# Turning the rows of the first and the last batch on TensorE in an attention and expert kernel, with new lists of the steps

## The chip, the cores and the metric

One core of a Trainium2 chip runs the whole program. Its engines each take their own queue of instructions in order: TensorE (PE, products; its loads of stationary data are PEld), VectorE (DVE), ScalarE (ACT), GpSimd (POOL) and the sync engine (SP), which issues DMAs. The metric is the device time of one execution in microseconds, the median of several runs.

## The reference

The input is 8 batches of 512 rows of 256 values in float32. A linear attention (no softmax, so keys and values can be multiplied first) and a mixture of experts each stand between two layer norms:

```
x = x + ln(attn(ln(x)))
    qkv = x @ Wqkv.T + b                 # 32 heads of 8
    ctx = q @ (k.T @ v) per head, then a group norm per head over (8, 512)
    return ctx @ out_w.T + out_b
x = x + ln(ffn(ln(x)))
    ffn(x) = silu(x @ gate.T) * (x @ up.T) @ down.T      # 704 hidden
    shared expert on all rows + top 2 of 8 experts by softmax(x @ gate_w.T)
```

## The kernel before

Products of float32 values are made from halves in float16: each operand is scaled and kept as a high and a low part, and three products (high x high, high x low, low x high) are summed (TERMS). TensorE wants the summed dimension on the partitions, so normalised rows have to be turned. For that ScalarE writes the high part of a batch's rows and VectorE the low part (steps turn1 and turn2, into rows1 and rows2), and SP issues four transposing DMAs (L421 into xq for the attention, L429 into xhl_v for router and shared expert).

The program has three stages. **START and eight rounds**: START computes batch 0's keys, values and state and its attention, and the first half of batch 1. Round b, for b from 1 to 6, goes through ORDER: the second half of batch b (ctx, group norm, out, lno, x2, ln2, turn2, logits), the first half of batch b + 1 (ln1_stats, ln1_apply, turn1, q, kv, state; FIRST_HALF), the shared expert for batch b - 1 (two tiles of 256 rows, each with six chunks: G is gate and up on TensorE, H the silu, product and split on ScalarE and VectorE, D down on TensorE), and the layout of expert b's weights from float32 (prep_max to prep). LAST_ORDER is round 7, without a first half and with routing steps. **TAIL** holds the shared expert for batch 7 and the routing: ranks (route_slots, route_order, route_positions), one-hot rows (one_hots on VectorE and GpSimd) that TensorE multiplies into index lists (invert), and route_indices. **Routed tiles**: 39 tiles of 256 gathered rows. GpSimd gathers (gather_x), SP turns (turn_x, L493), TensorE works, ScalarE copies out (y_out, L709), GpSimd scatters with addition (L628). Finished batches are normalised between the tiles; the last one after them.

What sets the order is the lists, written out by hand: every engine runs through the same PROGRAM and emits only its own part of each step, so the lists set each queue, and semaphores hold the engines together. G of chunk n waits until VectorE has made the product of chunk n - 2 (h_made, two PSUM banks), D of chunk n until its low half is there (lo_made), which VectorE makes in H of chunk n + 1. Attention has four PSUM banks (BANK); bank_ready waits for the last reader. In round b SP issues in this order: xres, turn1(b + 1), the store of x2, the store of a shared tile, turn2(b), the store of rows2 to xn2_d, the load of the next x, the next weights. xhl_v has two places by the parity of the batch: the tile xhl for odd ones and a part of the free weight slot 7 (spare) for even ones. xhl is also the place of the turned gathered tiles (xt16).

## Time and profile before

| | us |
|---|---|
| median of 3 runs (885.25 to 888.62) | 886.62 |
| the profiled execution | 888.74 |
| its span, first to last instruction | 887.0 |
| TensorE busy | 787.4 |
| VectorE busy | 586.4 |
| ScalarE busy | 483.7 |
| GpSimd busy | 291.1 |

The profile is of one execution. Busy time is summed per engine; the rows further down tell when each was busy, what an engine waited for, and the granted clock of TensorE, 1.00 being its high level.

### The profile page before, as it was taken

Reading aid. Unit: us, or ns where it says so; the run is one execution under the profiler, and the core shown is the slowest. Engines: PE = TensorE matmul, PEld = TensorE weight load, DVE = VectorE, ACT = ScalarE, POOL = GpSimd, SP = SyncE. Lnnn points to the kernel's source line nnn. Section 1 sums busy time; section 2 is a strip of 40 time slices with the busy share of each in tenths; the row PEclk is TensorE's granted clock in tenths of the full one; section 3 lists DMA queues with packets and bytes.
Section 4 is the critical chain, followed back from the end, with each engine's and each line's share of the span. In section 5 each row is a group of like instructions: output and inputs, shape, how many; then the busy total and the mean of one; then the engine's idle time right before and its main releaser. Section 6 shows DMA issues by size and latency. Waiting matters only on the chain.

```text
span 887.0 us, 21062 instructions
## 1 busy us (share of the span) xinstructions
PE 787.4 (89%) x6573; PEld 634.3 (72%) x6574; DVE 586.4 (66%) x1579; ACT 483.7 (55%) x1056; POOL 291.1 (33%) x316
## 2 busy tenths in 40 slices
PE   0757999999999999667799999999999999999990
PEld 0334767777666767545578888888888888888880
DVE  7163888888978887899477644455555555555552
ACT  1225575766656576622365655555555555656561
POOL 3010101010001000025245555555555555555532
PEclk9977999999999999979899999999999999999995
DMA  5125344536262625340324457766454646464723
GB/s 193 43 66 174 76 132 143 160 108 203 66 208 61 208 66 179 84 119 13 79 55 74 74 96 74 120 75 144 72 143 72 143 74 143 75 142 73 145 36 89
DMA packets 124307, 95.35 MB, mean 107 GB/s; under 512 B 85504, under 2 KB 115968, under 8 KB 123072
## 3 DMA queue, kind: packets, MB, share of 16 engines
q1 hardware_dynamic: 109264, 73.70, 30.6%
q0 software_dynamic: 14976, 20.78, 15.9%
q8 instruction: 39, 0.64, 0.3%
q14 instruction: 28, 0.23, 0.1%
HBM read 48.70 MB, written 27.39 MB: 86 GB/s over the span
## 4 chain that ended last, share of the span: by engine, by line
PE 72%; DVE 13%; DMA 4%; SPq 3%; ACT 3%; issue 3%; POOL 1%; ACTq 0%; DVEq 0%; POOLq 0%
PE ps L856 40%; PE ps L871 19%; PE ps L952 4%; SPq L429 3%; PE ps L911 2%; PE ps L937 2%; PE ps L917 2%; DVE mx L1173 2%; DVE hf L1144 2%; DMA wgu<-wgu 1%; DVE hT L1154 1%; DVE wdn L1440 1%; DMA xhl<-wgu 1%; DMA acc_d<-ysb,gst 1%; DVE st L1124 1%
## 5 line engine op out<-in xcount | busy, mean ns | idle before, releaser
L856 PE MATMUL ps<-xhl,wgu 128*128 128x256 f16 x3102 | 388.0, 275 | 12.3 <-DVE hf L1144 6.4
L856 PEld LDWEIGHTS ps<-xhl,wgu 128*128 (+1 forms) x3102 | 304.3, 99 | 55.0 <-issue 9.7
L1144 DVE SCALAR_TENSOR_TENSOR hf<-ps,sc,silu 128x256 f32<-128x256 f32 x330 | 159.6, 484 | 198.0 <-ACT silu L679 142.4
L871 PE MATMUL ps<-wdn,hT 128*128 (+1 forms) x1870 | 253.9, 274 | 1.6 <-DVE hT L1154 1.2
L679 ACT ACTIVATE silu<-ps,sc 128x256 f32<-128x256 f32 x275 | 130.1, 474 | 221.3 <-PE ps L856 206.9
L871 PEld LDWEIGHTS ps<-wdn,hT 128*128 128x128 f16 x1870 | 182.4, 98 | 25.7 <-DVE hT L1154 1.7
L628 POOL DMA_INDIRECT acc_d<-ysb,gst x78 | 128.7, 1650 | 44.5 <-POOL gst L624 30.9
L561 POOL TENSOR_TENSOR rstd<-ve,mhalf 128x4 f32<-128x4 f32 (+1 forms) x32 | 31.2, 974 | 322.2 <-DVE ve L1129 168.4
L693 ACT CAST hT<-hf 128x256 f16<-128x256 f32 x275 | 109.6, 398 | 17.9 <-DVE hf L1144 16.6
L1154 DVE TENSOR_TENSOR hT<-hf,hT 128x256 f16<-128x256 f32 x275 | 115.0, 418 | 1.7
L617 POOL DMA_INDIRECT attw<-xn_d,gst x78 | 80.8, 1035 | 44.5 <-POOL gst L613 32.6
L856 PE MATMUL ps<-wgu 128*128 128x256 f16 x528 | 64.8, 276 | 5.2 <-DVE hf L1144 5.2
L856 PEld LDWEIGHTS ps<-wgu 128*128 128x128 f16 x528 | 51.4, 100 | 16.6 <-DVE hf L1144 6.2
L917 PE MATMUL ps<-attw,att 128*128 128x512 f16 x192 | 47.0, 381 | 0.0
L624 POOL COPY gst<-ones 128x2 int32 (+1 forms) x39 | 8.5, 219 | 105.7 <-ACT ysb L709 105.7
L952 PE MATMUL ps<-attw,att 128*128 128x256 f32 x128 | 37.2, 415 | 3.1 <-DVE att L1335 3.1
L682 ACT ACTIVATE silu<-ps,sc 64x256 f32<-64x256 f32 x55 | 25.7, 468 | 25.9 <-PE ps L856 24.1
L911 PE MATMUL ps<-att,attw 128*128 128x512 f16 x96 | 26.3, 432 | 14.4 <-DMA att<-wdn 14.4
L709 ACT ACTIVATE ysb<-ps,yw 128x256 f32<-128x256 f32 x78 | 32.7, 472 | 3.4 <-DMA acc_d<-ysb,gst 3.4
L917 PEld LDWEIGHTS ps<-attw,att 128*128 128x128 f16 x192 | 17.9, 98 | 18.9 <-issue 0.8
L1204 DVE SCALAR_TENSOR_TENSOR wgu<-wgu,pw 128x1408 f16<-128x1408 f32 x16 | 26.4, 1682 | 7.0 <-ACT wgu L727 7.0
L753 ACT ACTIVATE att<-ps,colg 128x512 f32<-128x512 f32 x32 | 21.6, 684 | 15.5 <-PE ps L922 15.5
(227 smaller groups left out, 745.8 us busy)
## 6 DMA issues: line engine op xcount, KB each, us to landing
wgu<-in_gu SPq DMA_DIRECT2D x8, 1408.0 KB, 6.2
att<-in_x SPq DMA_DIRECT2D x16, 512.0 KB, 5.2
wdn<-in_dn SPq DMA_DIRECT2D x8, 768.0 KB, 8.3
x_d<-att SPq DMA_DIRECT2D x8, 512.0 KB, 3.0
xn_d<-wgu SPq DMA_DIRECT2D x8, 512.0 KB, 3.4
acc_d<-ysb SPq DMA_DIRECT2D x16, 256.0 KB, 3.2
att<-x_d SPq DMA_DIRECT2D x8, 512.0 KB
att<-acc_d SPq DMA_DIRECT2D x8, 512.0 KB, 4.4
```

The costliest lines, as they stand in the source:

```text
L617: g.indirect_dma_start(xg[:, r, t, :], None, xn2_d[:, :], bass.IndirectOffsetOnAxis(ap=idxc[:, 2 * r + t:2 * r + t + 1], axis=0)).then_inc ...
L628: g.indirect_dma_start(acc_d, bass.IndirectOffsetOnAxis(ap=idxc[:, 4 + t:5 + t], axis=0), ysb[:, t * D:(t + 1) * D], None, compute_op=ALU. ...
L679: a.activation(silu[:, c % 2 * TW:(c % 2 + 1) * TW], gu_ps[c % 2][:, 0:TW], ACT.Silu, scale=scale_of(slot, 0)).then_inc(silu_made, 1)
L693: a.copy(o, h).then_inc(hi_made, 1)
L709: ins = a.activation(ysb[:, tt * D:(tt + 1) * D], y_bank(u, tt), ACT.Copy, scale=by)
L856: ins = te.matmul(o, slot_gu(slot, hw, k, j), x(hx, k), start=(n == 0), stop=(n == len(TERMS) - 1))
L871: ins = te.matmul(y_bank(u, tt), h(hh), slot_dn(slot, c, hw), start=(c == 0 and n == 0 and tt == 0), stop=(c == FC - 1 and n == 1 and tt = ...
L911: ins = te.matmul(att_bank(QU + m)[:, :], wqkvT[:, hw, k, m * P:(m + 1) * P], xq[:, hx, k, :], start=(n == 0), stop=(n == len(TERMS) - 1))
L917: te.matmul(att_bank(KV_USES[t])[:, :], xq[:, hx, k, t * P:(t + 1) * P], wqkvT[:, hw, k, D:3 * D], start=(n == 0), stop=False)
L952: te.matmul(att_bank(OUT + h)[:, (t % 2) * D:(t % 2 + 1) * D], qT[:, k, t * P:(t + 1) * P], woT[:, k, :], start=(k == 0), stop=False)
L1144: v.scalar_tensor_tensor(out=hf[lo:P, c % 2 * TW:(c % 2 + 1) * TW], in0=up, scalar=scale_of(slot, 1, lo, P), in1=silu[lo:P, c % 2 * TW:(c ...
L1154: v.tensor_tensor(lo, h, hi, ALU.subtract).then_inc(lo_made, 1)
```

## The change

Batches 0 and 1 in the first norm (PE_FIRST) and batches 0 and 7 in the second (PE_SECOND) are turned by TensorE: eight transposes of 128x128 float32 blocks into two PSUM banks (turn, TURN1 and TURN2). ScalarE then writes the high and VectorE the low part from PSUM straight into xq (step turn1_out) or xhl_v (step xhl). The rows in float16 are still made for batch 0 and 7's second norm (step rows2, the former turn2), since xn2_d needs them, but no transposing DMA is issued. The other batches are turned by DMAs as before. The two places of xhl_v are swapped, so batch 7 is in the weight slot; the one-hot rows oh_hi move behind it. turn_x of the first two tiles now waits only for the gate and up products up to tile 13 of the shared expert, and the store of shared tile 15 goes behind them. The load of the last batch's sums is issued in two halves with a semaphore each. In a routed tile y_out is issued ahead of the normalising step of the same chunk, and in the last tile one chunk earlier. All four lists are new.

```
-ORDER = [("ctx",), ("G", 0), ("ctx_out",), ("channel_stats",), ("G", 1), ("H", 0), ("group_mean",), ("H", 1), ("G", 2), ("group_var",),
-         ("H", 2), ("D", 0), ("ctx_norm",), ("ln1_stats",), ("G", 3), ("G", 4), ("out",), ("H", 3), ("G", 5), ("ln1_apply",), ("H", 4),
-         ("D", 1), ("G", 6), ("turn1",), ("D", 2), ("H", 5), ("lno_stats",), ("G", 7), ("H", 6), ("D", 3), ("H", 7), ("lno_apply",),
...
+ORDER = [("ctx",), ("ctx_out",), ("G", 0), ("channel_stats",), ("H", 0), ("G", 1), ("group_mean",), ("G", 2), ("H", 1), ("ln1_stats",),
+         ("H", 2), ("group_var",), ("D", 0), ("G", 3), ("H", 3), ("ln1_apply",), ("D", 1), ("ctx_norm",), ("D", 2), ("G", 4), ("turn1",),
+         ("G", 5), ("out",), ("H", 4), ("H", 5), ("G", 6), ("D", 3), ("G", 7), ("prep_max", 0), ("G", 8), ("lno_stats",), ("H", 6),
+         ("q",), ("lno_apply",), ("q_out",), ("x2",), ("H", 7), ("kv", 0), ("H", 8), ("D", 4), ("kv_out", 0), ("D", 5), ("ln2_apply",),
...
+
+def turned_before(b, by_pe):
+
+    n = sum(c < b for c in by_pe)
+    return n, b - n
...
-CTX, GMEAN, GVAR, OUT, QU, STATE, LOGIT = 0, 2, 3, 4, 8, 16, 17
+CTX, GMEAN, GVAR, OUT, TURN1, QU, TURN2, STATE, LOGIT = 0, 2, 3, 4, 6, 8, 14, 16, 17
 KV_USES = [10, 11, 12, 13]
-BANK = {CTX: 0, CTX + 1: 1, GMEAN: 2, GVAR: 3, OUT: 0, OUT + 1: 1, QU: 2, QU + 1: 3,
-        10: 0, 11: 1, 12: 2, 13: 3, STATE: 2, LOGIT: 3}
-USES_FIRST = [QU, QU + 1] + KV_USES + [STATE]
+BANK = {CTX: 0, CTX + 1: 1, GMEAN: 2, GVAR: 3, OUT: 0, OUT + 1: 1, TURN1: 2, TURN1 + 1: 3, QU: 2, QU + 1: 3,
+        10: 0, 11: 1, 12: 2, 13: 3, TURN2: 0, TURN2 + 1: 1, STATE: 2, LOGIT: 3}
...
-        xhl_v = [a.rearrange("p (h k s) -> p h k s", h=2, k=KD) for a in (spare[:, 0:2 * KD * S], xhl[:, :])]
+        xhl_v = [a.rearrange("p (h k s) -> p h k s", h=2, k=KD) for a in (xhl[:, :], spare[:, 0:2 * KD * S])]
...
-                if b < B - 1:
+                if b < B - 1 and b + 1 not in PE_FIRST:
                     turn1(b + 1)
...
-                turn2(b)
+                if b in PE_SECOND:
+                    sp.wait_ge(rows2_made, b + 1)
+                else:
+                    turn2(b)
...
-            turn1(0)
...
-            for u in range(2):
-                store_shared(2 * B - 2 + u)
+            store_shared(2 * B - 2)
...
-                sp.wait_ge(gu_done, FC * (2 * B + max(i - 1, 0)))
+                sp.wait_ge(gu_done, FC * (2 * B - 2 if i < 2 else 2 * B + i - 1))
...
             for i in range(NTILE):
                 turn_x(i)
+                if i == 1:
+                    store_shared(2 * B - 1)
...
-            sp.dma_start(y_end, batch_rows(acc_d, B - 1)).then_inc(acc_end_loaded, 16)
+            for h in range(2):
+                sp.dma_start(y_end[:, 2 * h:2 * h + 2], batch_rows(acc_d, B - 1)[:, 2 * h:2 * h + 2]).then_inc(acc_end_loaded[h], 16)
...
+                if kind == "turn1_out" and b + 1 in PE_FIRST:
+                    for k in range(KD):
+                        use_done(act, b, TURN1 + k)
+                        a.activation(xq[:, 0, k, :], att_bank(TURN1 + k)[:, :], ACT.Copy, scale=X_SCALE).then_inc(xq_hi, 1)
...
+                if kind == "xhl" and b in PE_SECOND:
+                    wait(act, gu_done, 2 * FC * (b - 1))
+                    for k in range(KD):
+                        use_done(act, b, TURN2 + k)
+                        a.activation(xhl_v[b % 2][:, 0, k, :], att_bank(TURN2 + k)[:, :], ACT.Copy, scale=X_SCALE).then_inc(hi_x_made, 1)
...
-            def routed(i, r, slot, before, b=None, n=0):
+            def routed(i, r, slot, before, b=None, n=0, out_at=3):
...
+            def turn(b, n, rows, made, count):
+                pe.wait_ge(made, count)
+                for k in range(KD):
+                    bank_ready(pe, b, n + k)
+                    for t in range(NT):
+                        ins = te.transpose(att_bank(n + k)[:, t * P:(t + 1) * P], rows[:, t, k * P:(k + 1) * P], ident[:, :])
+                    ins.then_inc(att_done, 1)
 
...
+                if kind == "turn1_out" and b + 1 in PE_FIRST:
+                    for k in range(KD):
+                        dve.wait_ge(xq_hi, KD * turned_before(b + 1, PE_FIRST)[0] + k + 1)
+                        v.scalar_tensor_tensor(out=xq[:, 1, k, :], in0=att_bank(TURN1 + k)[:, :], scalar=X_SCALE, in1=xq[:, 0, k, :],
+                                               op0=ALU.mult, op1=ALU.subtract).then_inc(xq_lo, 1)
...
-            dve.wait_ge(acc_end_loaded, 16)
             dve.wait_ge(x2_end_loaded, 16)
             for h in range(2):
+                dve.wait_ge(acc_end_loaded[h], 16)
```

Here y_out in routed moves ahead of mid, with out_at=2 in the last tile. Two places show what the lists do. On TensorE, the end of START (batch 0): keys and values of batch 1 (L917, L922; L981, L986), the state (L929; L993), the logits (L966; L1032), ctx of batch 1 (L937; L1001) and the first two gate-ups (L856; L910). Before:

```order
L917 MATMUL ps<-attw,att 128x512 x6
L922 MATMUL ps<-attw 128x128 x4
L929 MATMUL ps<-att 128x128 x8
L966 MATMUL ps<-idx,wgu 128x8 x24
L937 MATMUL ps<-att,state 128x512 x2
L856 MATMUL ps<-wgu 128x256 x24
```

and now:

```order
L981 MATMUL ps<-attw,att 128x512 x6
L986 MATMUL ps<-attw 128x128 x4
L951 MATMUL ps<-ident,att 128x128 x8
L993 MATMUL ps<-att 128x128 x8
L1032 MATMUL ps<-idx,xhl 128x8 x24
L1001 MATMUL ps<-att,state 128x512 x2
L910 MATMUL ps<-xhl,wgu 128x256 x24
```

The turn (L951) stands ahead of the state, and the logits read what VectorE made from it. The second place is VectorE's queue in round 3, from H of chunk 1 on: hf is H's product, hT its low half, L1325 and L1328 (now L1396 and L1399) group_var, L1331 to L1335 ctx_norm, BN_STATS to ve the step ln1_stats (L1124 to L1129, now L1190 to L1195). Before:

```order
L1144 SCALAR_TENSOR_TENSOR hf<-ps,sc,silu 128x256
L1154 TENSOR_TENSOR hT<-hf,hT 128x256
L1325 SCALAR_TENSOR_TENSOR gst<-ps,gst 128x2
L1328 TENSOR_SCALAR ve<-gst 128x2
L1144 SCALAR_TENSOR_TENSOR hf<-ps,sc,silu 128x256
L1154 TENSOR_TENSOR hT<-hf,hT 128x256
L1331 TENSOR_TENSOR gst<-rstd,colg 128x2
L1332 TENSOR_TENSOR gst<-gst 128x2
L1333 TENSOR_TENSOR gst<-colg,gst 128x2
L1335 TENSOR_SCALAR att<-att,gst 128x512 x2
L1124 BN_STATS st<-att 128x6 x4
L1127 BN_AGGR mv<-st 128x2 x4
```

and now:

```order
L1210 SCALAR_TENSOR_TENSOR hf<-ps,sc,silu 128x256
L1220 TENSOR_TENSOR hT<-hf,hT 128x256
L1190 BN_STATS st<-att 128x6 x4
L1193 BN_AGGR mv<-st 128x2 x4
L1195 TENSOR_SCALAR ve<-mv 128x4
L1210 SCALAR_TENSOR_TENSOR hf<-ps,sc,silu 128x256
L1220 TENSOR_TENSOR hT<-hf,hT 128x256
L1396 SCALAR_TENSOR_TENSOR gst<-ps,gst 128x2
L1399 TENSOR_SCALAR ve<-gst 128x2
L1210 SCALAR_TENSOR_TENSOR hf<-ps,sc,silu 128x256
L1220 TENSOR_TENSOR hT<-hf,hT 128x256
L1199 TENSOR_SCALAR att<-att,mv,rstd 128x256 x4
```

ln1_stats moved from behind ctx_norm to a place between H1 and H2; ctx_norm now follows H3 and ln1_apply (L1199), behind the rows shown.

## Rows read from the trace of the kernel before

**Rows 1.** Stages: bounds in us, length, busy us of each engine (records), granted clock, DMA.

```profile
0.00:84.16 84.16, 43.36 (x200) 21.44 (x202) 40.78 (x115) 24.79 (x35) 12.87 (x30) 0.89 0.33 104
84.16:337.94 253.78, 249.92 (x1947) 181.73 (x1945) 217.35 (x568) 164.78 (x316) 22.33 (x24) 0.99 0.46 135
126.27:167.77 41.50, 41.48 (x332) 30.54 (x329) 36.08 (x96) 27.02 (x53) 3.72 (x4) 1.00 0.49 146
337.94:418.79 80.85, 58.72 (x491) 45.53 (x488) 70.75 (x248) 34.42 (x73) 18.15 (x19) 0.90 0.34 100
430.65:865.16 434.51, 429.60 (x3902) 381.40 (x3902) 250.17 (x629) 253.51 (x619) 228.50 (x232) 1.00 0.53 95
```

**Rows 2.** Timeline of the start: start us, us, engine, line, operation, [idle before, releaser].

```profile
14.24 1.37 DVE L1133 TENSOR_SCALAR att<-att,mv,rstd 128x256 f32<-128x256 f32 x4
...
25.71 5.30 PE L911 MATMUL ps<-att,attw 128*128 128x512 f16 x12 [10.94 <-DMA att<-wdn]
```

**Rows 3.** Timelines of TensorE and ScalarE: forms like the new ones.

```profile
14.39 0.38 PE L902 MATMUL ps<-ident,attw 128*18 128x128 f32 x1 [3.91 <-DVE attw L1093]
...
38.71 2.05 PE L929 MATMUL ps<-att 128*128 128x128 f32 x16 [0.78 <-ACT att L753]
...
37.97 0.69 ACT L753 ACTIVATE att<-ps,colg 128x512 f32<-128x512 f32 x1 [1.04 <-PE ps L922]
```

**Rows 4.** Timeline of VectorE around ln1_stats in batch 3.

```profile
176.95 1.40 DVE L1124 BATCH_NORM_STATS2 st<-att 128x6 f32<-128x256 f32 x4
...
178.87 0.48 DVE L1144 SCALAR_TENSOR_TENSOR hf<-ps,sc,silu 128x256 f32<-128x256 f32 x1
```

**Rows 5.** Timelines of GpSimd, ScalarE and TensorE: end of batch 0, ctx of two batches.

```profile
59.68 1.01 POOL L561 TENSOR_TENSOR rstd<-ve,mhalf 128x4 f32<-128x4 f32 x1 [10.08 <-DVE ve L1129]
66.25 2.37 POOL L561 TENSOR_TENSOR rstd<-ve,mhalf 128x4 f32<-128x4 f32 x1 [5.56 <-DVE ve L1129]
...
68.91 2.07 ACT L775 ACTIVATE att<-att,attw,rstd 128x256 f32<-128x256 f32 x4 [2.03 <-DVE attw L1355]
...
79.74 0.80 PE L966 MATMUL ps<-idx,wgu 128*128 128x8 f16 x24 [2.47 <-DMA wgu<-wgu]
80.40 3.76 PE L937 MATMUL ps<-att,state 128*128 128x512 f32 x4
...
126.27 1.96 PE L937 MATMUL ps<-att,state 128*128 128x512 f32 x4
```

**Rows 6.** Waits of TensorE for the logits' input (us in total, times, longest), and SP's transposes.

```profile
PE ps L966 <- DMA wgu<-wgu: 4.5, 3, 2.5
PE ps L966 <- DMA xhl<-wgu: 4.2, 2, 3.7
...
160.38 5.12 SPq L429 DMA_TRANSPOSE wgu<-wgu  x4
...
202.02 5.67 SPq L429 DMA_TRANSPOSE xhl<-wgu  x4
```

**Rows 7.** Chain of work that ended last, from 845 us on: start us, us, what.

```profile
848.03 1.31 PE ps L856 x12
...
859.71 0.73 ACT ysb L709 x2
...
863.50 3.74 DMA acc_d<-ysb,gst
...
874.77 4.45 DMA att<-acc_d
```

**Rows 8.** Timelines of GpSimd and SP between the indices and the routed tiles.

```profile
421.54 0.96 POOL L617 DMA_INDIRECT attw<-xn_d,gst  x1 [0.30 <-issue]
...
426.63 17.37 SPq L493 DMA_TRANSPOSE xhl<-attw  x6
```

**Rows 9.** DMA issues of the page: KB each, median us to landing.

```profile
acc_d<-ysb SPq DMA_DIRECT2D x16, 256.0 KB, 3.2
```

**Rows 10.** The chain at ctx of batch 5.

```profile
252.80 3.29 PE ps L937 x4
```

126 lines of the change are left out of this document (82 added, 44 removed), and 17 rows, old and new, of tables (LAST_ORDER, ORDER, TAIL).

## The prediction

> **What bounds the kernel now.** I read the stage table first (busy time by stretch, cut where the work of TensorE changes kind), then each engine's timeline at the cuts. It shows four different limits [rows 1]. From 0 to 84.16 us nothing covers batch 0's chain from load to routed input, and TensorE is busy for 43 of 84 us. From 84.16 to 337.94 six batches run with TensorE busy nearly throughout: 253.8 us, 42.3 each, the best 41.5. From 337.94 to 418.79 VectorE is busy 70.75 of 80.85 us and TensorE only 58.72: the routing and VectorE's own queue bound it. 11.86 us pass from the indices to the first routed tile. Then 434.51 us of routed tiles are full TensorE work, and the last 21.84 us are a chain of transfers and small operations. The profiled execution took 888.74 us, 1.74 outside its 887.0 us span and 2.1 above the median of 886.62; the sum is made against 888.74 and its difference laid on the median.
>
> **Part 1, turning by TensorE in the start.** Before, batch 0's normalised rows are ready at 15.61, then a copy, a subtraction (late, behind the weights on VectorE) and four transposes that SP issues lead to q at 25.71, after 10.94 us of TensorE's waiting [rows 2]. Now eight 128x128 float32 transposes follow at 15.65. Nothing in the trace has that form 128 wide; one transpose with 18 columns of stationary data took 0.38 us alone, eight plain float32 products of that shape took 2.05 in 16 records [rows 3]. So eight cost between 1.0 (8 records of 0.128) and 3.07 (8 x 0.38); I take 2.05, the row of the same shape. ScalarE then reads a 512-wide PSUM bank in 0.69, VectorE subtracts in about 0.7 (an estimate: 256 columns from PSUM take 0.48 [rows 4]). First bank 16.7, ScalarE 17.4; VectorE is held by the weights and by the bias turn, which TensorE now reaches only behind the eight, until about 18.4; second ScalarE copy 18.4; two subtractions, 19.8. q starts near 20.0 in place of 25.71: **-5.7** (5.1 to 6.2).
>
> In batch 0's middle two things push back. The first norm's apply (1.3 us) now stands ahead of ctx_norm on VectorE, +0.4, and the eight transposes of batch 1 stand ahead of "out" on TensorE, another +0.6 (0 to 1.6). VectorE also lays out two weight pieces before the statistics of "out", but "out" ends later than they do. Against it stands GpSimd's root, 2.37 us with a weight piece running beside it on VectorE and 1.01 seven us earlier without one [rows 5]; that piece is moved away, -1.35. ScalarE's kv_out of tile 2 now stands before ln2_apply and gives about +0.4. I call the middle zero, with 1.5 either way.
>
> The second norm: ln2_apply ends at 70.98. Before, one copy, one subtraction, four SP issues and a landing bring the logits to 79.74 and, behind ctx, the first shared gate-up to 84.16; ctx ran at the low clock level, 3.76 us against 1.96 in a later batch [rows 1, 5]. Now: eight transposes to 73.0, copies and subtractions as above to 74.6, the state (2.05) from 73.1 to 75.15, logits to 75.9, ctx to 77.7 at the high level or 79.6 at the low one. The last weight piece waits on VectorE behind the subtractions, the masked state and the rows for the scratch tensor (1.2 us), until 77.9. So gate-up 0 starts 6.3 earlier on top of q's gain (4.5 if ctx runs low). Together **-12.5** (-9.5 to -15). Covers that vanish: the SP queue is empty either way.
>
> One rule speaks against this. TensorE ran ctx at the low level right after its 2.47 us wait for the turned rows [rows 5]. The Trainium skill, "TensorE: Matmul & The Clock Gate", section "Part 4: PE-mode transpose", says that transposes do not bring the high clock level and gives about 275 ns for one of 128x128 in a kernel (bfloat16). By that figure a turn would be an estimated 2.2 us, which changes this sum by 0.2, and ctx would run low, which is the -4.5 above; no row here can show the rule. It is the second rival.
>
> **Part 2, the six batches.** Their turns stay with the DMAs; order and buffers change. Before, the turned rows arrive just as TensorE asks for the logits: of five waits there (8.7 us) 2.5 is batch 0's and 3.7 batch 7's, the other three are 2.5 together [rows 6]. The new list puts the copy to rows2 earlier and one down step behind the logits. That removes most of these. But VectorE's queue in the first third now reads H1, ln1_stats, H2, group_var, H3, ln1_apply, ctx_norm. From ctx at T: channel statistics end at T+4.4, H0 and group_mean at 5.3, H1 (0.40+0.40) at 6.1; ln1_stats then holds the queue 1.92 us, from 176.95 to the next hf at 178.87 in the row of before [rows 4], to 8.0; H2 ends at 8.8. TensorE, through G2, group_var, D0 and G3 (1.31 us for 12 products, half of it for 6, 0.1 for group_var [rows 7]), stands before D1 at 8.2 and waits 0.6 for H2's low half; D2 waits 0.5 for H3's; "out" waits 0.2 for ctx_norm (T+12.8), which stands behind ln1_apply (1.29). Sum 1.3 us per batch. Before, ctx_norm stood ahead of ln1_stats and G3, G4 ahead of D1, so it had no wait there. Behind "out" the list has room; the turned rows then land at about T+41.3 (rows2 at 33.6, 5.1 of issue [rows 6], 2.5 of landing), which fits logits at T+41.4. TensorE's own work is 41.3 (the best batch of before was 41.5 [rows 1]), so a batch is 42.6, and those whose transposes hold SP for 5.7 us, as at 202.02, instead of 5.1 [rows 6] reach 43.2: 42.9 against 42.3. Batch 1 keeps its table load. **+3.3**, from -3 (no wait) to +8.
>
> **Part 3, last batch and tail.** TensorE's turn of batch 7 takes away 3.7 us of waiting for logits [rows 6]. But VectorE sets the indices. Its queue gains two PSUM subtractions (1.4) and one H more ahead of route_indices (0.8), and idles less: walking both lists with the durations of the trace I find 6 us of idle before and 4 now. **0**, +-3.
>
> **Part 4, indices to first routed tile.** SP stands in y_out's store until 426.5 and turns the gathered tile from 426.63, although its second gather was issued at 421.54 [rows 8]. The swap frees xhl two tiles earlier, and the store of tile 15 goes behind both turns. An indirect transfer that adds took 3.74 us from issue to landing [rows 7]; so the gather is there by 425.3 at the latest, 424.7 with the 3.2 of a plain 256 KB transfer [rows 9]. **-1.6** (-1.3 to -1.9). The store is then issued behind four transposes, and gather 2 waits for it; that gather is needed only at routed tile 2, two tiles of 11 us later.
>
> **Part 5, routed tiles and end.** 0 for the tiles: the copy out moves by 0.6 us on ScalarE, which is not what TensorE waits for. In the last tile it goes from 859.71 to about 857.45, so the scatter lands at 865.0, not 867.23; the last copy can start when TensorE is done at 865.16: 865.2 for 867.3, -2.1 [rows 7]. The load of 4.45 us becomes two halves: 3.2 for the first (256 KB row), the second by 4.85; its statistics start there instead of at +5.7, and the first shift follows 0.6 earlier [rows 7, 9]. **-2.7**.
>
> **Sum**: -12.5 +3.3 +0 -1.6 +0 -2.7 = -13.5; 888.74 gives 875.2, the median **873.1**.
>
> **Rivals.** (a) *The new list holds*: H1 to H3 run in VectorE's gaps and batches cost 41.8: -3 in place of +3.3, 866.8. For it: VectorE is busy for only 217 of 254 us there [rows 1]. Against: an engine takes its queue in order, and the wait follows from that order. (b) *Cold turns*: the turns cost 3.07 each and leave the clock low: start -9.5, and the batches 43.2: 878. For it: the low level after 2.47 us of waiting. (c) *Slower*: the three short waits in a batch do what a late transpose did ahead of 252.80: some 1.6 us of waiting, then ctx at the low level, 3.29 for 1.8, together 3 us [rows 6, 10]. In six batches that is 18 on top of the 1.3 x 6 = 8 of the waits, 26 in place of 3.3: 896. It ends above the present time if each batch loses more than 2.8 us to it. Against: after the short wait ahead of 126.27 ctx ran at the high level, 1.96 us, and that batch at a granted clock of 1.00 [rows 1, 5]. (d) *Routing later*: the one-hot steps of GpSimd or VectorE slip in the new TAIL by 5 us, and half of the start's gain is lost: about 884, no change. (e) *The turns gain little, since slot 0's weights end last*: those stand at 77.9 in the sum, so it is in it.
>
> **Numbers.** Forecast 0.50; (a) 0.18; (b) 0.17; (d) 0.08; (c) 0.04; 0.03 for better than (a). Range 864 to 881.5 (start and batches at their bounds together reach further, but not at once). What a measurement can tell here is 0.5%, 4.4 us: faster than 882.2 has 0.90, no change 0.06, slower than 891.1 0.04.
>
> **What would show it.** q near 20.0, "out" near 46.6, gate-up 0 near 71.7, next ctx starts every 42.6 to 43.2 with waits of about half a microsecond before D1 and D2 released by VectorE; indices about 80.9 after the last ctx; first routed tile 10.3 after the indices; last copy out 0.1 behind TensorE. Batches of 41.5 would refute part 2, TensorE records of more than 0.38 per transpose part 1, and a last stage that grows would mean that VectorE's queue was walked wrongly.

## The result, and the profile after the change

The changed kernel takes **874.14 us** (median of 4 runs, 873.57 to 875.29) beside 886.36 us of the kernel before on the same chip: a ratio of 0.9859, 95% interval 0.9839 to 0.9879. The forecast was 873.1 in a range of 864.0 to 881.5. The profiled execution took 874.38 us with a span of 872.6; the forecast on that scale was 875.2.

The table cuts both spans at the same events. "Indices" is GpSimd's copy of them (418.86 before, 410.23 after).

| stretch | before | after | difference | forecast |
|---|---|---|---|---|
| start to the first shared gate-up | 84.16 | 70.68 | -13.5 | -12.5 |
| from there to the last batch's ctx | 253.78 | 256.15 | +2.4 | +3.3 |
| that ctx to the indices | 80.92 | 83.40 | +2.5 | 0 |
| indices to the first routed tile | 11.79 | 9.90 | -1.9 | -1.6 |
| routed tiles | 434.51 | 433.94 | -0.6 | 0 |
| behind TensorE's last product | 21.84 | 18.53 | -3.3 | -2.7 |
| span | 887.0 | 872.6 | -14.4 | -13.5 |

The stages of the kernel after, as in [rows 1] (bounds, length, busy time of PE, PEld, DVE, ACT and POOL, granted clock, DMA share and GB/s):

```profile
0.00:70.68 70.68, 43.53 (x224) 23.66 (x225) 42.06 (x119) 26.05 (x40) 12.40 (x30) 0.95 0.22 81
70.68:326.83 256.15, 249.20 (x1946) 179.85 (x1947) 216.17 (x568) 163.38 (x314) 22.25 (x24) 1.00 0.47 140
112.25:155.17 42.92, 41.87 (x328) 30.10 (x327) 36.56 (x96) 27.45 (x54) 3.71 (x4) 1.00 0.47 140
326.83:410.23 83.40, 61.17 (x520) 47.14 (x518) 73.52 (x252) 37.86 (x80) 18.25 (x20) 0.96 0.28 88
420.13:854.07 433.94, 429.74 (x3902) 382.06 (x3902) 248.66 (x629) 253.94 (x619) 228.71 (x232) 0.99 0.51 96
```

The stretches differ by 14.4 us and the medians by 12.2, since the profiled execution of the kernel before was 2.4 us above its median; the parts add up to the larger number. In the kernel before the bound at 84.16 lies at the end of ctx, which the first gate-up record (83.95) overlaps; from start to start the first stretch is 13.3 us shorter.

In the start TensorE's busy time is that of before (43.53 for 43.36 us); 13.7 us of idle time are gone. In the inner batches it is the idle time that has grown: 256.15 - 249.20 = 6.95 us for 3.86.

The timeline of TensorE in the start, which answers to [rows 2, 3, 5]:

```profile
15.66 1.97 PE L951 MATMUL ps<-ident,att 128*128 128x128 f32 x8 [5.20 <-DVE att L1199]
...
19.52 5.30 PE L975 MATMUL ps<-att,attw 128*128 128x512 f16 x12 [1.67 <-DVE att L1361]
...
44.23 1.97 PE L951 MATMUL ps<-ident,att 128*128 128x128 f32 x8 [1.74 <-DVE att L1199]
45.99 1.91 PE L1016 MATMUL ps<-attw,att 128*128 128x256 f32 x4
...
65.15 1.10 PE L951 MATMUL ps<-ident,att 128*128 128x128 f32 x8 [1.02 <-ACT att L830]
66.08 1.95 PE L993 MATMUL ps<-att 128*128 128x128 f32 x16
67.87 0.75 PE L1032 MATMUL ps<-idx,xhl 128*128 128x8 f16 x24
68.62 1.98 PE L1001 MATMUL ps<-att,state 128*128 128x512 f32 x4
```

A turn is eight transposes in eight records. The first two, behind waits of 5.20 and 1.74 us (the second ends a stretch in which TensorE mostly waited), took 1.97 us each; the third, behind 1.02 us, took 1.10. Behind the third turn the state, the logits and ctx follow with no wait, and ctx runs at the high level (1.98 us) where it took 3.76 [rows 5].

Waits of TensorE in one inner batch (112.25 to 155.17; us in total, times, longest); there are no others, and none at the logits:

```profile
PE ps L925 <- DVE hT L1220: 0.7, 2, 0.4
PE ps L1005 <- DVE gst L1385: 0.4, 1, 0.4
```

Between the indices and the routed tiles, and at the end (GpSimd, SP's queue, TensorE, VectorE), beside [rows 7, 8]:

```profile
410.23 0.19 POOL L658 COPY gst<-idx 128x2 int32<-128x2 int32 x1 [6.74 <-DVE idx L1538]
...
415.68 7.22 SPq L535 DMA_TRANSPOSE xhl<-attw  x4
...
420.13 1.23 PE L910 MATMUL ps<-xhl,wgu 128*128 128x256 f16 x5 [6.67 <-DMA xhl<-attw]
...
861.71 0.80 SPq L563 DMA_DIRECT2D att<-acc_d  x2
...
864.92 0.75 DVE L1567 BATCH_NORM_STATS2 st<-att 128x6 f32<-128x256 f32 x2 [10.28 <-DMA att<-acc_d]
```

### The profile page after: what moved, and what is told of

Read it like the earlier page. It is cut to its first block, busy times and chain, and to the rows that moved or that the text cites. A ratio compares the mean times of both kernels' runs of the same rounds, so it can differ in the third digit from the quotient of the medians.

```text
span 872.6 us, 21123 instructions
## 1 busy us (share of the span) xinstructions
PE 785.9 (90%) x6605; PEld 634.1 (73%) x6606; DVE 586.8 (67%) x1585; ACT 486.2 (56%) x1062; POOL 290.8 (33%) x316
## 4 chain that ended last, share of the span: by engine, by line
PE 72%; DVE 17%; ACT 5%; issue 3%; DMA 2%; POOL 1%; ACTq 0%; SPq 0%; DVEq 0%; POOLq 0%
PE ps L910 40%; PE ps L925 18%; PE ps L981 5%; PE ps L1016 3%; DVE wgu L1270 3%; PE ps L975 2%; DVE hf L1210 2%; ACT wgu L772 2%; DVE wdn L1270 1%; PE ps L986 1%; DVE hT L1220 1%; DVE st L1382 1%; DVE wdn L1515 1%; PE ps L1020 1%; ACT silu L724 1%
## 5 line engine op out<-in xcount | busy, mean ns | idle before, releaser
L910 PE MATMUL ps<-xhl,wgu 128*128 128x256 f16 x3102 | 384.9, 274 | 12.7 <-DMA xhl<-attw 6.7
L910 PEld LDWEIGHTS ps<-xhl,wgu 128*128 (+1 forms) x3102 | 302.7, 98 | 54.5 <-issue 8.6
L925 PEld LDWEIGHTS ps<-wdn,hT 128*128 128x128 f16 x1870 | 179.8, 98 | 40.6 <-DVE hT L1220 13.4
L738 ACT CAST hT<-hf 128x256 f16<-128x256 f32 x275 | 109.4, 398 | 14.4 <-DVE hf L1210 11.8
L910 PE MATMUL ps<-wgu 128*128 128x256 f16 x528 | 65.4, 277 | 4.2 <-DVE hf L1210 4.2
L910 PEld LDWEIGHTS ps<-wgu 128*128 128x128 f16 x528 | 51.1, 100 | 14.8 <-DVE hf L1210 4.2
L981 PE MATMUL ps<-attw,att 128*128 128x512 f16 x192 | 47.2, 382 | 1.8 <-ACT att L814 1.8
L981 PEld LDWEIGHTS ps<-attw,att 128*128 128x128 f16 x192 | 18.4, 99 | 20.7 <-ACT att L814 2.3
L1222 DVE TENSOR_TENSOR hT<-hf,hT 64x256 f16<-64x256 f32 x55 | 23.2, 422 | 9.8 <-ACT hT L741 7.0
```

What stands on the lines that cost most here:

```text
L738: a.copy(o, h).then_inc(hi_made, 1)
L910: ins = te.matmul(o, slot_gu(slot, hw, k, j), x(hx, k), start=(n == 0), stop=(n == len(TERMS) - 1))
L925: ins = te.matmul(y_bank(u, tt), h(hh), slot_dn(slot, c, hw), start=(c == 0 and n == 0 and tt == 0), stop=(c == FC - 1 and n == 1 and tt = ...
L981: te.matmul(att_bank(KV_USES[t])[:, :], xq[:, hx, k, t * P:(t + 1) * P], wqkvT[:, hw, k, D:3 * D], start=(n == 0), stop=False)
```

## The experiments

The theory was the forecast's own: the three turns give what their waits cost (Part 1), the new list's place of ln1_stats costs what Part 2 says, the routing is bound by VectorE (Part 3), and the two small edits give Parts 4 and 5. The rival throughout: the gain is in the new lists and the turns are off the path. Ratios are to the kernel before, timed on the same chip; its medians were 886.4 to 888.8 us in the four comparisons, so only ratios are compared. The changed kernel's is 0.9859; 0.0011 of a ratio is 1 us. Each ratio is good to about 0.002, and a difference of two of them to about 0.003, which is 2.5 us (an estimate from the intervals): e5 and e11 are within that, e6b barely outside.

| run | ratio | 95% interval | against 0.9859, us |
|---|---|---|---|
| e1_first0_dma | 0.9928 | 0.9911 to 0.9944 | +6.1 |
| e2_second0_dma | 0.9956 | 0.9939 to 0.9972 | +8.6 |
| e3_second7_dma | 0.9915 | 0.9899 to 0.9932 | +5.0 |
| e4_stats_back | 1.0059 | 1.0042 to 1.0077 | +17.7 |
| e5_old_last | 0.9864 | 0.9843 to 0.9885 | +0.4 |
| e3b_second7_dma | 0.9929 | 0.9907 to 0.9950 | +6.2 |
| e7_turn_even | 0.9927 | 0.9907 to 0.9946 | +6.0 |
| e8_old_order | 0.9813 | 0.9788 to 0.9837 | -4.1 |
| e9_old_start | 1.0068 | 1.0044 to 1.0093 | +18.5 |
| e11_first1_dma | 0.9886 | 0.9867 to 0.9906 | +2.4 |
| e6b_head_end_old | 0.9888 | 0.9867 to 0.9909 | +2.6 |
| e10_old_lists_dma7 | 0.9782 | 0.9765 to 0.9798 | -6.8 |

Two profiled executions of one program differ, too: batch 0's ctx started between 33.8 and 35.5 us in the kernels whose start up to it is the same, the stretch from the last ctx to the indices took 83.4 to 85.1 in those that have the changed kernel's lists and turn there, and the routed stage, the same work in all, 433.7 to 436.7. Differences are therefore read within a stretch, from an event of the same trace. One stretch needs more care. With the changed kernel's start, an early ctx of batch 0 (33.8 to 34.1 us: e4, e5, e6b, e8, e10) was followed by the next one after 34.9 us and a late one (35.1 to 35.5: the changed kernel, e3, e3b, e7) after 33.1 to 33.3, so that batch 1's ctx came at 68.2 to 69.0 in all of them. In the early kind TensorE reached its high level sooner in batch 0's q and in the o projection, and fell back in the k products of batch 1. There a run is compared with its own kind.

### The three turns of the start, one at a time

```diff
-PE_FIRST, PE_SECOND = (0, 1), (0, B - 1)
+PE_FIRST, PE_SECOND = (1,), (0, B - 1)      # e1, and SP's turn1(0) back
+PE_FIRST, PE_SECOND = (0, 1), (B - 1,)      # e2, rows2 right behind ln2_apply
+PE_FIRST, PE_SECOND = (0,), (0, B - 1)      # e11
```

**e1.**


> The changed kernel with one part undone: the rows of batch 0 of the first norm are turned by DMAs again, as in the kernel before; the rest is as changed. Theory (the forecast's Part 1): the turn stands on the path, so that batch 0's q starts near 25.5 us again instead of 19.5 (25.71 before), everything behind it moves by about 5.9 us, and the median is 879 to 881 instead of 874.1. Rival: the first weights' preparation and the start's other steps would be late anyway, or the gain at the start came from the new start list and not from the turn; then gate-up 0 moves by under 2 us and the median stays under 876.5.

Batch 0's ctx moved from 35.45 to 41.30 us, gate-up 0 from 70.68 to 76.56, and the time by 6.1 us. The whole of this turn stands on the path, and the theory's number holds.

**e2.**


> The changed kernel with the rows of batch 0 of the second norm turned by DMAs again (the rows of the second norm are split right behind the norm's last step, as before); the rest is as changed. Theory (the forecast's Part 1): a wait of about 4.5 us for the turned rows comes back ahead of the logits and the clock is at its lower level behind it; gate-up 0 starts at 76 to 78.5 us instead of 70.68, median 879.5 to 882. Rival: the middle of the start (the o projection, q, k and v of batch 1) has slack for the turn, so that it moves by under 2 us, below 876.5.

It cost 8.6 us. The wait is there, and with it the low clock, which began ahead of it: the state already ran at the low level (3.66 us for 1.95), behind a wait of 2.68 us. TensorE of e2, then the stage from that ctx to the next in e2 and, third row, in the changed kernel:

```profile
67.16 3.66 PE L993 MATMUL ps<-att 128*128 128x128 f32 x16 [2.68 <-ACT att L803]
74.34 0.80 PE L1032 MATMUL ps<-idx,xhl 128*128 128x8 f16 x24 [3.52 <-DMA xhl<-wgu]
75.00 3.76 PE L1001 MATMUL ps<-att,state 128*128 128x512 f32 x4
```

```profile
75.00:121.23 46.23, 44.53 (x332) 31.31 (x330) 33.39 (x93) 27.06 (x51) 3.71 (x4) 0.94 0.45 129
```

```profile
68.62:112.25 43.63, 41.86 (x326) 30.08 (x326) 35.35 (x95) 27.12 (x52) 3.71 (x4) 1.00 0.49 147
```

Both stages have the same waits (1.0 and 0.7 us); the 2.6 us between them are TensorE's busy time at a granted clock of 0.94 in place of 1.00. The loss of 8.6 us is thus 6.1 from the norm's apply step to the logits (74.34 - 63.38 = 10.96 for 67.87 - 63.03 = 4.84), which is the DMA turn with its wait, and 2.6 behind it, two thirds of that in ctx itself and the rest in the products that follow.

**e11.**


> The changed kernel with the rows of batch 1 of the first norm (which are turned ahead of the o projection of batch 0) turned by DMAs again; the rest is as changed. Theory (the forecast's Part 1, the middle at 0 in 1.5): the DMA turn lies beside the group norm and the o projection, as before, and q of batch 1 doesn't wait; without the 1.97 us of transposes gate-up 0 comes within 1.5 us of where it is, 69.5 to 72, and the median is 873 to 876. Rival: e1 and e2 lost more than their waits, because the clock is lower behind a wait; here the wait is short but the o projection comes right behind the group norm's wait either way; a loss of 3 us or more, 877 or more, would say that the transposes keep the clock up there.

The forecast had called the middle zero; the ratios put 2.4 us on it, within their noise, and the trace shows the loss. Batch 1's ctx starts at 71.16 us, 2.2 to 2.9 later than in the nine kernels with the changed kernel's start. From batch 0's ctx (34.15, of the early kind) to it are 37.01 us, for 34.90 in e8, which is of that kind too: +2.1. TensorE, then VectorE, of e11:

```profile
46.99 2.08 PE L1016 MATMUL ps<-attw,att 128*128 128x256 f32 x4 [5.59 <-DVE att L1406]
```

```profile
44.20 1.23 DVE L1357 SCALAR_TENSOR_TENSOR wdn<-att,wdn 128x1024 f16<-128x1024 f32 x1 [1.12 <-ACT wdn L788]
```

and TensorE of e8:

```profile
44.73 1.91 PE L1016 MATMUL ps<-attw,att 128*128 128x256 f32 x4
...
55.85 1.77 PE L981 MATMUL ps<-attw,att 128*128 128x512 f16 x6 [2.46 <-ACT att L814]
```

In the place tried here the split of the rows stands ahead of ctx_norm on VectorE; in the kernel before it stood behind it. It waits 1.12 us for ScalarE's half and takes 1.23, and the o projection starts 12.84 us behind ctx and not 10.74 as in e8: +2.1, the whole loss. The clock moved time about and took none. In e11 three of the projection's four parts ran at the low level (2.08 us each), so that it and the step from it to q took 8.15 us for 5.90; but k and v of batch 1 then ran at the high level, and from q to the second norm's apply it took 10.44 us for 12.68. That the transposes keep the clock up is not shown either: in e9, of the late kind and with none ahead of the projection, it took 6.75 us, for 6.60 in the changed kernel.

### The start's list

The edit puts the whole list START of the kernel before back; the lines show the place of the second turn.

```diff
-(0, "ln2_apply"), (0, "kv", 3), (0, "turn2"), (0, "kv_out", 3), (0, "state"), (0, "xhl"), (0, "state_out"), (0, "rows2"), (0, "logits")
+(0, "ln2_apply"), (0, "turn2"), (0, "xhl"), (0, "rows2"), (0, "kv", 0), (0, "kv_out", 0), (0, "kv", 1)
```

**e9.**


> The changed kernel with the start's list of steps as in the kernel before; the turns of batches 0 and 1 stay on TensorE, each with its splits right behind it, where that list turned rows. Theory: the start's gain is the three turns, not the new list; q of batch 0 starts at 19.5 us, gate-up 0 at 70.7 to 73 us (70.68 with the new list), median 873.5 to 876.5. Rival: the new list, which puts two parts of the weights' preparation ahead of the o projection and the root of the second norm behind nothing else, carries some of it; gate-up 0 at 74 to 78, median 877 to 881.

Both were wrong, by far: gate-up 0 starts at 86.35 us, 15.7 us later than in the changed kernel and later than in the kernel before (84.16). TensorE of e9:

```profile
67.85 1.97 PE L950 MATMUL ps<-ident,att 128*128 128x128 f32 x8 [10.57 <-ACT att L829]
...
84.53 1.98 PE L1000 MATMUL ps<-att,state 128*128 128x512 f32 x4 [2.70 <-DVE state L1365]
```

The old list names the second turn right behind the norm's apply step and ahead of k and v of batch 1. As a DMA that cost nothing: SP's queue waited. As a product it stands in TensorE's own queue, waits 10.57 us for ScalarE, and 8 us of k and v products stand behind it, which in the changed kernel start 4.6 us behind q. The new list names it behind "kv" 3, where the wait is 1.02. From the turn to the state it is 11.34 us for 0.93, which makes 10.4 of the 15.7. Another 2.8 are between the state and ctx (5.34 for 2.54): the old list has the masked state last on VectorE, behind three weight pieces, and the wait of 2.70 for it is bare without the DMA's wait that covered it before. Most of the rest, 2.3, is between ctx and q, where the turn of batch 1 stands behind the o projection. So the turn and its place belong together: where the old list had its turn, the start gains nothing over before. The old list with the turn moved behind "kv" 3 wasn't tried.

### Turning where the DMAs are hidden

```diff
-PE_FIRST, PE_SECOND = (0, 1), (0, B - 1)
+PE_FIRST, PE_SECOND = (0, 1), (0, 2, 4, 6, B - 1)
-("kv", 3), ("G", 11), ("prep_scale",), ("H", 10), ("kv_out", 3), ("D", 7)
+("kv", 3), ("G", 11), ("turn2",), ("prep_scale",), ("H", 10), ("kv_out", 3), ("xhl",), ("D", 7)
```

**e7.**


> The changed kernel with TensorE also turning the rows of the second norm of batches 2, 4 and 6 (eight transposes each, and two more splits on ScalarE and VectorE), where the DMAs do it beside other work; batches 1, 3 and 5 are as changed and stand beside them in the same trace. Theory: in the inner batches TensorE is the bound and the DMA turn is hidden, so that a turned batch takes 1.0 to 1.6 us more than the 42.92 of its neighbours (1.10 us of transposes at the high clock, and splits beside them), 3 to 5 us in all, median 877 to 879. Rival 1: no difference over 0.4 us in a batch, 874 to 875.5. Rival 2: the added splits hold VectorE up behind them, over 2.5 us in a batch, median over 881.

It cost 6.0 us. The first of the batches turned (batch 2), and batch 3 behind it, which isn't:

```profile
111.86:155.65 43.79, 42.74 (x335) 30.97 (x334) 36.88 (x97) 27.53 (x55) 3.71 (x4) 1.00 0.40 127
155.65:199.56 43.91, 41.87 (x328) 30.08 (x326) 37.65 (x97) 28.34 (x55) 3.71 (x4) 1.00 0.44 133
```

The turned batch takes 0.87 us more than 42.92, all of it TensorE's busy time (42.74 for 41.87). The batch behind it takes 0.99 more with its busy time unchanged: its first wait has grown, by 0.98 us. As far as the rows show, that comes from VectorE's added splits at the end of the batch ahead.

```profile
150.66 1.29 DVE L1431 SCALAR_TENSOR_TENSOR xhl<-ps,xhl 128x512 f16<-128x512 f32 x2 [1.10 <-ACT xhl L819]
```

```profile
161.52 0.39 PE L1005 MATMUL ps<-gst,mask 128*128 128x4 f32 x2 [1.36 <-DVE gst L1385]
```

That wait was 0.37 to 0.38 in every batch of the changed kernel. A turn thus costs 1.9 us where it saves nothing, half of it in a batch that doesn't do it.

### The inner list

```diff
-("H", 1), ("ln1_stats",), ("H", 2), ("group_var",), ("D", 0), ("G", 3), ("H", 3), ("ln1_apply",), ("D", 1), ("ctx_norm",), ("D", 2)
+("H", 1), ("H", 2), ("group_var",), ("D", 0), ("G", 3), ("H", 3), ("D", 1), ("ctx_norm",), ("ln1_stats",), ("D", 2), ("ln1_apply",)
```

**e4.**


> The changed kernel; in the list of the inner batches the statistics of the next batch's first norm (1.4 us of VectorE and its small steps) stand behind the hidden tiles H2 and the context norm again instead of ahead of H2, and the norm's apply step behind D2. Theory (the forecast's Part 2): they hold VectorE ahead of what TensorE waits for; the waits of TensorE behind VectorE at the group mean (0.38), D1 (0.44) and D2 (0.23), 1.05 us in a batch, go or fall under 0.3 together, the inner batches take 41.9 to 42.2 instead of 42.92 and the median is 868 to 870.5. Rival 1: VectorE is short over the whole stretch, the waits only move behind the moved steps, and the batch stays at 42.6 or more. Rival 2: the apply step is late, the rows are turned too late for q, and the batch gets longer than 43.3.

The theory fell: a batch took 45.82 us, +2.9 each and 17.7 in all. VectorE in e4 and, third and fourth row, TensorE behind it:

```profile
130.40 1.39 DVE L1199 TENSOR_SCALAR att<-att,mv,rstd 128x256 f32<-128x256 f32 x4 [1.12 <-POOL rstd L606]
132.91 1.22 DVE L1357 SCALAR_TENSOR_TENSOR wdn<-att,wdn 128x1024 f16<-128x1024 f32 x1 [1.12 <-ACT wdn L788]
```

```profile
134.68 1.47 PE L910 MATMUL ps<-wgu 128*128 128x256 f16 x12 [1.08 <-DVE hf L1210]
...
139.97 0.28 PE L910 MATMUL ps<-wgu 128*128 128x256 f16 x1 [1.86 <-DVE hf L1210]
```

Statistics, GpSimd's root, the apply step, ScalarE's half and VectorE's half are a chain over three engines. With the steps close together VectorE waits out each hand-over (1.12 and 1.12 us) with the hidden tiles queued behind it, and TensorE waits for those: 1.08 + 1.86 = 2.94 us, which is the loss. The run moved both steps, so this is the price of the two together.

It also shows what D2 waits for. H3 on VectorE and D2 on TensorE in e4, then D1 and D2 in the changed kernel:

```profile
125.03 0.48 DVE L1210 SCALAR_TENSOR_TENSOR hf<-ps,sc,silu 128x256 f32<-128x256 f32 x1 [1.04 <-ACT silu L724]
```

```profile
125.90 0.83 PE L925 MATMUL ps<-wdn,hT 128*128 128x256 f16 x6 [0.85 <-DVE hT L1220]
```

```profile
121.56 0.83 PE L925 MATMUL ps<-wdn,hT 128*128 128x256 f16 x6 [0.45 <-DVE hT L1220]
122.61 0.83 PE L925 MATMUL ps<-wdn,hT 128*128 128x256 f16 x6 [0.23 <-DVE hT L1220]
```

Without the statistics ahead of H2, D1 has no wait, but D2 starts 10.36 us behind ctx in both kernels (125.90 - 115.54 and 122.61 - 112.25). H3's product starts 9.49 us behind ctx in both, in e4 after 1.04 us in which VectorE only waited for ScalarE's silu. So ln1_stats ahead of H2 only splits one wait in two; it fills time in which VectorE would stand, and D2 hangs on ScalarE's silu of chunk 3.

```diff
-ORDER = [("ctx",), ("ctx_out",), ("G", 0), ("channel_stats",), ("H", 0), ("G", 1), ("group_mean",), ("G", 2), ("H", 1), ("ln1_stats",),
+ORDER = [("ctx",), ("G", 0), ("ctx_out",), ("channel_stats",), ("G", 1), ("H", 0), ("group_mean",), ("H", 1), ("G", 2), ("group_var",),
...
+         ("rows2",), ("kv_out", 1), ("kv", 2), ("kv_out", 2), ("prep_spread",), ("prep_scale",), ("kv", 3), ("G", 11), ("kv_out", 3),
```

**e8.**


> The changed kernel with the list of the inner batches as in the kernel before (no inner batch turns rows on TensorE, so nothing else changes there). Inner batches took 42.92 us each in the changed kernel, with 1.05 us of TensorE's waits behind VectorE in each, and 41.4 to 43.1 (mean 42.3 over the five from ctx of batch 1) before, with almost no wait on record. e4 has shown that moving the statistics alone back makes it worse (45.8 us), so that the list must be taken as a whole. Theory: the old list gives 41.4 to 42.5 us a batch here too, the median is 869 to 872.5. Rival 1: the irregular batches before (43.1 twice) come from that list; mean 42.7 to 43.2, median 873 to 876. Rival 2: the old list depends on the old buffers; over 43.5 us a batch, over 877.

This one is faster than the changed kernel: ratio 0.9813. The batches took 43.52, 41.36, 42.00, 41.35 and 41.90 us, mean 42.03; the first two:

```profile
111.53:155.05 43.52, 41.95 (x332) 30.19 (x328) 37.99 (x97) 28.27 (x56) 3.71 (x4) 1.00 0.49 139
155.05:196.41 41.36, 41.34 (x332) 30.41 (x328) 35.36 (x95) 26.81 (x52) 3.71 (x4) 1.00 0.47 142
```

Its only waits of TensorE from there to the last ctx are DMA ones:

```profile
PE ps L1032 <- DMA xhl<-wgu: 1.4, 2, 1.2
PE ps L975 <- DMA att<-wdn: 0.3, 1, 0.3
```

The old list has batches with no wait at all, and now and then a late turn. The new one has no late turn and the same 1.05 us of waits every time. In the kernel before, a late turn let the clock fall once, behind a wait of 1.6 us (the ctx of [rows 10], 3.29 us); in e8, whose longest was 1.2, it stayed at 1.00 in every batch. Whether a late turn lets the clock fall is thus not a property of the list alone; what it takes, no run here shows.

### The last batch and the tail

```diff
-PE_FIRST, PE_SECOND = (0, 1), (0, B - 1)
+PE_FIRST, PE_SECOND = (0, 1), (0,)
-("ln2_apply",), ("route_top2", 0), ("H", 9)
+("ln2_apply",), ("rows2",), ("route_top2", 0), ("H", 9)
```

The last line is that of e3; e3b has `("ln2_apply",), ("route_top2", 0), ("rows2",), ("H", 9)`.

**e3.**


> The changed kernel with the rows of batch 7 of the second norm turned by DMAs again; the rest is as changed. Theory (the forecast's Part 3): VectorE's chain of routing steps sets when the indices are made, not the turn; from ctx of batch 7 to the indices it stays at 83.4 us within 0.7, and the median within 1 us of 874.1. Rival 1: the logits wait for the turn and the second half of the routing starts 2.5 to 4 us later, median 876.5 to 878. Rival 2: without the turn VectorE and ScalarE do fewer steps (two splits of 0.64 us) and the stretch falls back to the 80.9 us of the kernel before, 871.6.

**e3b.**


> As e3_second7_dma (batch 7's second norm turned by DMAs), but the split of its rows stands behind route_top2 and not ahead of it: there VectorE waited 3.29 us for ScalarE's half of the split, with the routing steps and the hidden tile H9 behind it. Theory: the 6.5 us that e3 lost are 4.3 us of that placement and about 2 us of the later turn, so that the stretch from ctx of batch 7 to the indices comes down from 89.6 us to 84.5 to 86.5 (83.4 with the turn on TensorE), median 876 to 878. Rival 1: the turn itself is what e3 paid for (the logits come 5 us later in either placement); the stretch stays at 88.5 or more, median 879.5 to 881.5. Rival 2 (the forecast's Part 3): the turn is off the path; 83 to 84 us, median 873.5 to 875.

Neither held the forecast's zero: 89.9 us from ctx to the indices in e3, 88.8 in e3b, for 83.40. e3 stood VectorE still for ScalarE's half of the split, with route_top2 and a hidden tile behind it (VectorE, TensorE):

```profile
357.68 1.23 DVE L1435 SCALAR_TENSOR_TENSOR wgu<-att,wgu 128x1024 f16<-128x1024 f32 x1 [3.29 <-ACT wgu L824]
```

```profile
364.64 1.46 PE L910 MATMUL ps<-xhl,wgu 128*128 128x256 f16 x6 [6.25 <-DVE hf L1210]
```

e3b takes that away and gets only 1 us of it back in its trace and nothing in the ratios (+6.2 for +5.0, within their noise), because now the turned rows are late (waits of TensorE, then of VectorE, e3b):

```profile
PE ps L1032 <- DMA wgu<-wgu: 4.5, 1, 4.5
```

```profile
DVE hf L1210 <- ACT silu L727: 7.7, 2, 6.4
```

With the new lists the turn by DMA costs 5 to 6 us in either place. ScalarE takes the logits out (logits_out) ahead of H 11, so VectorE stands 6.4 us at H 11, and route_probs 1 behind it needs the logits too. In the old lists H 11 stands ahead of logits_out, and route_top2 0, 5 us of VectorE, ahead of route_probs 1. e5 has the whole of the two old lists; the line shows where the turn stands in them:

```diff
-         ("turn2",), ("G", 10), ("xhl",), ("H", 10), ("rows2",), ("G", 11), ("D", 8), ("logits",), ("D", 9), ("logits_out",), ("D", 10),
+         ("route_top1", 0), ("G", 7), ("G", 8), ("H", 8), ("turn2",), ("D", 4), ("xhl",), ("rows2",), ("D", 5), ("H", 9), ("G", 9),
```

**e5.**


> The changed kernel with the lists of the last batch and of the routing tail as in the kernel before; the turn of batch 7's second norm stays on TensorE (its two splits stand behind D4 of that list). From ctx of batch 7 to the indices the kernel before takes 80.9 us and the changed one 83.4. Theory: the 2.5 us more come from the new lists alone, which put hidden tiles ahead of routing steps on VectorE; with the old lists and TensorE's turn the stretch is 78 to 81 us, median 870 to 873.5. Rival: they come from the turn with its two added splits (0.64 us of VectorE and 0.54 us of ScalarE each, twice); the stretch is 82.5 to 84.5 us, median 873.5 to 876.

The stretch took 83.71 us, where the same lists with the DMA turn took 80.92 before; the rival holds, and the new last lists are not the cause (the stage of e5):

```profile
327.16:410.87 83.71, 61.44 (x495) 47.11 (x494) 73.20 (x250) 36.28 (x77) 18.36 (x19) 0.86 0.28 87
```

Counted from ctx, VectorE's channel statistics begin 0.64 us later than before (3.26 for 2.62; the batch ahead leaves its weights to be prepared), the next step behind the splits is 2.1 us later and the first one-hot step 2.55 (59.73 for 57.18). VectorE's two added splits are 1.28 of it. How much the inner list adds is open: e8, with the old inner list and the new last ones, begins its statistics at 2.71 and still takes 83.4 us, as the changed kernel does, and the old lists throughout with the turn on TensorE were not run.

### The two small edits

```diff
+            for u in range(2):
+                store_shared(2 * B - 2 + u)          # both ahead of turn_x(0)
...
-                sp.wait_ge(gu_done, FC * (2 * B - 2 if i < 2 else 2 * B + i - 1))
+                sp.wait_ge(gu_done, FC * (2 * B + max(i - 1, 0)))
...
-            for h in range(2):
-                sp.dma_start(y_end[:, 2 * h:2 * h + 2], batch_rows(acc_d, B - 1)[:, 2 * h:2 * h + 2]).then_inc(acc_end_loaded[h], 16)
+            sp.dma_start(y_end, batch_rows(acc_d, B - 1)).then_inc(acc_end_loaded[0], 16)
...
-                routed(i, i % 2, s1, True, b=B - 2, n=i - NTILE + 3, out_at=2 if i == NTILE - 1 else 3)
+                routed(i, i % 2, s1, True, b=B - 2, n=i - NTILE + 3, out_at=3)
```

**e6b.**


> The changed kernel with three small edits undone, which lie in different stretches of one trace: both stores of the last shared tiles stand ahead of the first routed tile's turn on the queue again and that turn waits for one more tile's gate and up (Part 4); the last tile but one goes out after chunk 3 and not 2, and the end's load is one transfer (Part 5). Theory: from the indices to the first routed tile 11.5 to 12 us instead of 9.90 (11.79 before); from TensorE's last matmul to the end's load 7.64 us stays (the scatters follow ScalarE's last copy) or grows to 9.6 as before; from the load's issue to the first statistics 4.47 us instead of 3.21; in all +3 to +5 us, median 877 to 879. Rival: the first routed tile waits for the gather itself, and the end for the scatter's landing, so that the edits give under 1.5 us together, under 875.6.

+2.6 us, and what the trace shows of it is at the end. GpSimd, SP's queue, TensorE, SP's queue and VectorE of e6b:

```profile
411.43 0.19 POOL L655 COPY gst<-idx 128x2 int32<-128x2 int32 x1 [7.70 <-DVE idx L1535]
...
416.97 7.00 SPq L535 DMA_TRANSPOSE xhl<-attw  x4
...
421.31 1.01 PE L907 MATMUL ps<-xhl,wgu 128*128 128x256 f16 x4 [6.65 <-DMA xhl<-attw]
...
866.03 0.32 SPq L560 DMA_DIRECT2D att<-acc_d  x1
...
870.47 0.75 DVE L1564 BATCH_NORM_STATS2 st<-att 128x6 f32<-128x256 f32 x2 [13.04 <-DMA att<-acc_d]
```

From the indices to the first routed tile it is 9.88 us with Part 4's edits and without them: in the new tail the last shared tile is done so early that its store (415.68) no longer holds SP. At the end, TensorE's last product (856.87) to the load is 9.16 us for 7.64, and the load to the first statistics 4.44 for 3.21: 1.52 + 1.23 = 2.75, about what the ratios give.

### A faster version

```diff
-PE_FIRST, PE_SECOND = (0, 1), (0, B - 1)
+PE_FIRST, PE_SECOND = (0, 1), (0,)
```

ORDER, LAST_ORDER and TAIL are those of the kernel before, with "rows2" where they had "turn2" (in LAST_ORDER, too, the step that splits the rows).

**e10.**


> What the runs so far point to: TensorE turns the rows of batches 0 and 1 at the start alone, with the new start list; the lists of the inner batches, of the last batch and of the tail are those of the kernel before, and batch 7's second norm is turned by DMAs as before. e8 (old inner list) measured 870.3 against 874.1 to 875 of the changed kernel. Theory: the old last lists with the DMA turn take 80.9 us from ctx of batch 7 to the indices, as before, where e5 (old last lists, TensorE's turn and its two added splits on VectorE) took 83.7; so 2 to 3 us below e8, 866.5 to 869. Rival: the shorter stretch is given back between the indices and the first routed tile (9.8 us with TensorE's turn, 11.8 before) or by a lower clock behind the wait for the turned rows, 869.5 to 871.5.

Ratio 0.9782 (0.9765 to 0.9798): 2.2% below the kernel before and 0.8% below the changed one, the fastest of all. From ctx to the indices and to the first routed tile (the stage, SP's queue, TensorE):

```profile
322.46:403.68 81.22, 60.30 (x491) 46.34 (x489) 71.27 (x248) 34.58 (x74) 18.32 (x20) 0.88 0.33 100
```

```profile
409.21 6.32 SPq L535 DMA_TRANSPOSE xhl<-attw  x4
...
413.58 7.67 PE L910 MATMUL ps<-xhl,wgu 128*128 128x256 f16 x48 [4.12 <-DMA xhl<-attw]
```

81.2 us, as the theory said, and 9.90 to the first routed tile. Here Part 4's edits seem to do their work, read from the queue alone, since the kernel without them was not run: the store is issued at 415.57, behind the turn, and in the kernel before it was issued ahead of it and held it [rows 8]. Against e8 the difference of the ratios is 0.0031, 2.7 us, with intervals that overlap by 0.001 (its upper end 0.9798, e8's lower 0.9788); the stretch in the two traces (81.2 for 83.4) agrees with it.

## Why the forecast was right, and where it was not

The mechanism of the main part held, and the total is closer than its parts. They missed by 5.9 us when added without their signs and by 0.9 with them: the start and the end gave more than was forecast, the last batch took it back. That offset is luck.

**Part 1 (-12.5, measured -13.5).** The forecast's own terms, 5.7 and 6.3, add up to 12.0; -12.5 went into its sum. q came 6.2 us earlier for 5.7: eight transposes took 1.97 us at the low level (2.05 taken), ScalarE's copies 0.60 and VectorE's subtractions 0.64 each (0.7 estimated). The middle was 0.3 us longer, from q to ln2_apply 43.51 for 43.20. From ln2_apply to gate-up 0 it was 7.65 for 15.25, -7.6 where the forecast had -6.3, mostly since the third turn took 1.10 us and not 2.05. e1 and e2 put 6.1 and 8.6 us on these two turns. Taking back the one that the forecast called free cost 2.1 us in e11's trace, by the place of the split ahead of ctx_norm; a place behind it, as before, wasn't tried. What the forecast did not see is that the gain hangs on the turn's place in TensorE's queue (e9).

**The clock (rival b).** Refuted: behind the third turn ctx ran in 1.98 us. The Trainium skill, "TensorE: Matmul & The Clock Gate", section "Part 4: PE-mode transpose", says that transposes do not bring the high level and take about 275 ns in one kernel's context (bfloat16). In this trace the turn behind a wait of 1.02 us took 1.10 us for eight float32 ones, 0.14 each, and 1.97 behind waits of 5.20 and 1.74, 0.25 each; the level was kept through eight of them, with k and v at the high level ahead. Whether transposes alone can raise it is open: behind the first turn and a wait of 1.67 us, q took 5.30 us in the changed kernel, as in the kernel before without a turn, and 4.08 to 4.52 in the kernels of the early kind.

**Rivals (a) and (c).** A batch took 42.92 us and not 41.8, so (a) fell in this list. Its three waits never let the clock fall: ctx took 1.88 us and the granted clock was 1.00 in each of the five batches, which refutes (c).

**Part 2 (+3.3, measured +2.4).** The number held: 42.92 us in each of five batches, in the forecast's 42.6 to 43.2, with 0.38 at the group mean, 0.44 before D1 and 0.23 before D2. It is made of two misses: TensorE's own work was 41.87 us and not 41.3, and the waits 1.05 and not 1.3, with one at the group mean that the forecast lacked and none at "out". And the cause was half wrong. ln1_stats ahead of H2 does make D1 wait, but not D2 later: D2 starts 10.36 us behind ctx with it and without it (e4), since ScalarE's silu sets H3. What the list as a whole costs, e8 shows: 0.9 us a batch against the old one in the same kernel.

**Part 3 (0, measured +2.5).** Inside its bounds, but mis-sized, and by the forecast's own sign (a last stage that grows) VectorE's queue was walked wrongly. The forecast let 2.2 us of added work on VectorE vanish in 2 us less of idle time. VectorE's busy time grew by 2.8 us (73.52 for 70.75), and its idle time in the stage fell by 0.2 (9.9 for 10.1). The last lists are not the cause (e5); the turn's two splits are 1.28 us of it, and the rest is not parted. In the old lists a wait for batch 7's logits (3.2 us in e10) lies behind VectorE, as the forecast said; in the new ones it does not (e3, e3b).

**Part 4 (-1.6, measured -1.9).** Right in size. In the changed kernel either cause is enough: the store had been done early in the new tail (e6b), or it stands behind the turn (e10).

**Part 5 (-2.7, measured -3.3).** e6b puts 2.75 on it, but in other shares: the last copy out gave 1.5 for 2.1, and the split load 1.2 for 0.6. The first half landed 3.2 us behind its issue, as forecast, and the second was no longer waited for.
